# A context covariance and a value projection computed inside the third attention, and root tables loaded ahead of their use

## The reference

```python
x = x + _L2_xattn_ref(_layernorm(x), ctx_768, ctx_768, ...)   # 16 heads of 8
x = x + _L2_ffn_ref(_layernorm(x), ...)                       # top 2 of 8 experts
x = x + _L3_xattn_ref(_layernorm(x), ctx_768, ...)
...
def _L3_xattn_ref(q, k, Wq, Wk, Wv, Wo):
    query = q @ Wq.T
    key_p = k @ Wk.T
    value = k @ Wv.T
    sim = jnp.einsum('bqd,bkd->bqk', query, key_p)
    mean = jnp.mean(sim, axis=(1, 2), keepdims=True)
    var = jnp.var(sim, axis=(1, 2), keepdims=True)
    sim = (sim - mean) * jax.lax.rsqrt(var + EPS)
    attn = jax.nn.softmax(sim, axis=-1)
    out = jnp.einsum('bqk,bkd->bqd', attn, value)
    return out @ Wo.T
```

## Time and profile before

| | us |
|---|---|
| median of 3 runs (lowest to highest) | 3944.25 (3941.36 to 3946.58) |
| the profiled execution | 3943.8 |
| its span | 3942.1 |
| TensorE busy | 3643.4 (92%) |
| ScalarE busy | 2589.0 (66%) |
| VectorE busy | 1717.8 (44%) |
| GpSimd busy | 465.9 (12%) |

### The profile page before, as it was taken

How to read it: one execution, slowest core, us unless ns; L and a number is a source line. 1 busy time by engine, 2 the same in 40 slices (tenths; PEclk the granted TensorE clock), 3 DMA queues, 4 the chain that set the end, 5 groups by cost and what they waited for, 6 DMA issues and landing times.

```text
span 3942.1 us, 83687 instructions
## 1 busy us (share of the span) xinstructions
PE 3643.4 (92%) x30692; PEld 1378.2 (35%) x30692; DVE 1717.8 (44%) x1661; ACT 2589.0 (66%) x2756; POOL 465.9 (12%) x1844
## 2 busy tenths in 40 slices
PE   7999999999899999999999999868888888798989
PEld 4333333345433333333333333421111111455444
DVE  4222222223377777777777777710000000543344
ACT  5999999973355655555555555479999999102321
POOL 1222222210000000000000000012222222100210
PEclk8999999999899999999999999989999999898989
DMA  5323232212111111111111100140101000100000
GB/s 179 102 78 101 80 99 82 95 72 64 51 33 38 43 37 38 37 42 39 38 37 41 40 27 1 43 121 4 38 3 38 3 3 1 47 21 1 0 12 27
DMA packets 109875, 183.11 MB, mean 46 GB/s; under 512 B 23700, under 2 KB 46896, under 8 KB 107408
## 3 DMA queue, kind: packets, MB, share of 16 engines
q1 hardware_dynamic: 109584, 178.75, 14.8%
HBM read 107.13 MB, written 71.57 MB: 45 GB/s over the span
## 4 chain that ended last, share of the span: by engine, by line
PE 71%; ACT 12%; issue 11%; DVE 4%; ACTq 1%; DMA 0%; SPq 0%; POOLq 0%; DVEq 0%; POOL 0%
PE ps L672 18%; PE ps L697 18%; ACT probs L1014 12%; PE ps L463 7%; PE ps L451 4%; PE ps L432 3%; PE ps L576 3%; PE ps L555 2%; PE ps L830 2%; PE ps L841 2%; PE ps L437 2%; PE ps L889 2%; PE ps L903 1%; PE ps L562 1%; PE ps L257 1%
## 5 line engine op out<-in xcount | busy, mean ns | idle before, releaser
L1014 ACT ACTIVATE probs<-ps 128x1024 f32<-128x1024 f32 x1632 | 1512.4, 1083 | 60.3 <-PE ps L451 60.1
L1111 ACT ACTIVATE probs<-ps 128x1024 f32<-128x1024 f32 x816 | 836.4, 1025 | 596.4 <-PE ps L672 583.5
L1743 DVE TENSOR_TENSOR vbuf<-vbuf,probs 128x1024 f32<-128x1024 f32 (+1 forms) x800 | 972.9, 1223 | 335.5 <-ACT probs L1111 335.5
L463 PE MATMUL ps<-probs,vst 128*32 128x512 f32 x6528 | 864.8, 602 | 137.5 <-ACT probs L1014 137.3
L451 PE MATMUL ps<-qz,kst 32*128 32x512 f32 x3264 | 415.3, 495 | 25.8 <-issue 19.9
L451 PEld LDWEIGHTS ps<-qz,kst 32*128 32x128 f32 x3264 | 162.6, 182 | 712.7 <-issue 689.3
L1264 POOL CAST kst<-kb 128x128 fp32r x816 | 241.9, 296 | 1289.2 <-PE ps L463 1178.2
L1570 DVE COPY qs<-ps 128x512 f32<-128x512 f32 (+1 forms) x208 | 141.6, 681 | 574.3 <-PE ps L437 285.2
L672 PE MATMUL ps<-probs,kb 64*64 64x512 f32 x2560 | 332.3, 589 | 0.0
L1609 DVE COPY work<-ps 128x512 f32 x16 | 11.1, 692 | 694.9 <-PE ps L463 694.9
L672 PE MATMUL ps<-probs,qz 64*64 64x512 f32 x2048 | 269.8, 594 | 8.2 <-issue 7.9
(11 more groups left out here) (366 smaller groups left out, 3091.9 us busy)
## 6 DMA issues: line engine op xcount, KB each, us to landing
kv_scratch<-qs SPq DMA_DIRECT2D x192, 256.0 KB, 2.0
kb<-k_scratch SPq DMA_DIRECT2D x24, 816.0 KB, 7.3
kb<-kv_scratch SPq DMA_DIRECT2D x72, 256.0 KB, 2.9
qz<-kv_scratch SPq DMA_DIRECT2D x64, 256.0 KB, 2.9
k_scratch<-klo SPq DMA_DIRECT2D x24, 512.0 KB, 3.4
vbuf<-in_L_ffn_W SPq DMA_DIRECT2D x32, 256.0 KB, 3.1
klo<-kv_scratch SPq DMA_DIRECT2D x32, 256.0 KB, 2.9
qs<-kv_scratch SPq DMA_DIRECT2D x24, 256.0 KB, 3.0
```

The source lines that it names most:

```text
L463: mm = pe.matmul(ps[32 * j:32 * j + 32, 6 + half, :], vst[:, r, 32 * j:32 * j + 32], probs[:, r, j * HT:(j + 1) * HT], start=start, stop=stop)
L1014: act.activation(probs[:, r, b * T:(b + 1) * T].rearrange("p (h n) -> p h n", h=2), ps[:, 2 * buf:2 * buf + 2, :], ACT.Exp, scale=HD8 ** - ...
L1111: act.activation(pr1[:, (u + 2 * odd) % 4], ps[:, 2 * b:2 * b + 2, :], ACT.Exp, scale=HD64 ** -0.5)\
L1743: dve.tensor_tensor(sum1[0:k, odd, h], sum1[0:k, odd, h], e, ALU.add).then_inc(s["added"], 1)
```

## The change

Three things are done.

1. The mean of the context is spread in step 3 of half 6 of the third attention (the first half of the last group of heads). VectorE copies and subtracts it there, in three pieces of 17, 17 and 16 tiles and one of 4 rows, and GpSimd does so no longer. TensorE computes the covariance in steps 16 to 48 of the same half, one or two tiles in a step, each as three matmuls with 32 columns of weights, in bank 7. The load of the context is issued by SyncE after the queries of half 7, and `cn2` lies in the buffer of keys that the last group doesn't use.
2. The value projection is computed in half 7, in 26 parts of up to 256 context rows, each tile as four matmuls with 32 columns of weights, in bank 6; VectorE copies the 13 chunks out, where ScalarE did so.
3. `load_table(5, ACT.Sqrt)` stands at six further places of ScalarE's program, behind the exps and activations that use other tables.

Beside this the loop over the groups of the third attention is unrolled in TensorE's and VectorE's programs.

```diff
+COV_FROM = 16
+COV_AT = [COV_FROM + k * (ST - 2 - COV_FROM) // ST for k in range(ST)]
+V3_PARTS = 2 * NC
+V3_AT = [RING, RING] + [2 * RING + k * (ST - 2 * RING) // (V3_PARTS - 2) for k in range(V3_PARTS - 2)]
...
+CENTRED = 2 * NG - 2
...
-        cmean = flat[:, 5 * T:5 * T + C]
+        cmean = klo[:, 0, 0:C]
...
-        cn2 = vbuf[:, 2 * T:2 * T + ST * C].rearrange("p (t c) -> p t c", t=ST)
+        cn2 = kbf[:, 0:ST * C].rearrange("p (t c) -> p t c", t=ST)
...
-        vp = vbuf[:, 0:ST * P]
+        vp = kbf[:, 0:ST * P]
...
+                def context_mean(gh):
+
+                    pe.wait_ge(s["den_copied"], gh + DENS[layer])
+                    pe.wait_ge(s["x_ready"], 4)
+                    pe.matmul(ps[:, 7, 0:P], stat[:, 0:1].to_broadcast([P, P]), ident[:, :], start=True, stop=True)\
+                        .then_inc(s["cmean_ready"], 1)
+
+                def covariance(t):
+
+                    pe.wait_ge(s["ccent_ready"], min(3, t // PIECE + 1) if t < SF else 4)
+                    k = P if t < SF else TAIL
+                    for j in range(C // 32):
+                        cut = slice(32 * j, 32 * j + 32)
+                        mm = pe.matmul(ps[cut, 7, 0:C], cn2[0:k, t, cut], cn2[0:k, t, :], start=(t == 0), stop=(t == ST - 1))
+                    if t == ST - 1:
+                        mm.then_inc(s["cov_ready"], 1)
+
+                def values3(gh, c, p0, p1):
...
+                    if c == 0 and p0 == 0:
+                        pe.wait_ge(s["den_copied"], gh + DENS[layer])
+                    if c and p0 == 0:
+                        pe.wait_ge(s["v3_copied"], c)
+                    for u in range(p0, p1, P):
+                        for j in range(G):
+                            cut = slice(32 * j, 32 * j + 32)
+                            mm = pe.matmul(ps[cut, 6, u:u + P], ctxT[0:C, c0 + u + 32 * j:c0 + u + 32 * j + 32], wT[0:C, 3, :],
+                                           start=True, stop=True)
...
+                        elif g * 2 + half == CENTRED + 1:
+                            pe.wait_ge(s["cov_copied"], 1)
...
+                            elif gh == CENTRED:
+                                if t == RING:
+                                    context_mean(gh)
+                                for k in range(ST):
+                                    if COV_AT[k] == t:
+                                        covariance(k)
+                            elif gh == CENTRED + 1:
+                                for k in range(V3_PARTS):
+                                    if V3_AT[k] == t:
+                                        values3(gh, k // 2, k % 2 * (HT // 2), (k % 2 + 1) * (HT // 2))
...
-            pe.matmul(ps[:, 5, 0:P], stat[:, 0:1].to_broadcast([P, P]), ident[:, :], start=True, stop=True)\
-                .then_inc(s["cmean_ready"], 1)
...
             exps8(0)
+            load_table(5, ACT.Sqrt)
             layernorm(1)
...
             exps8(2)
+            load_table(5, ACT.Sqrt)
             layernorm(5)
...
+            load_table(5, ACT.Sqrt)
             experts8(1)
...
             exps1(3, mode3, 0, stat[:, 12:13])
+            load_table(5, ACT.Sqrt)
             layernorm(8)
...
-            pool.wait_ge(s["in_ctx2"], 32)
-            pool.wait_ge(s["cmean_copied"], 1)
-            pool.tensor_tensor(cn2[:, 0:SF, :], cn2[:, 0:SF, :], cmean.unsqueeze(1).to_broadcast([P, SF, C]), ALU.subtract)\
-                .then_inc(s["ccent_ready"], 1)
-            pool.tensor_tensor(cn2[0:TAIL, SF, :], cn2[0:TAIL, SF, :], cmean[0:TAIL], ALU.subtract).then_inc(s["ccent_ready"], 1)
...
+                def centred_context():
+
+                    dve.wait_ge(s["cmean_ready"], 1)
+                    dve.tensor_copy(cmean, ps[:, 7, 0:C]).then_inc(s["cmean_copied"], 1)
+                    dve.wait_ge(s["in_ctx2"], 32)
+                    dve.wait_ge(s["cmean_copied"], 1)
+                    for t0 in range(0, SF, PIECE):
+                        t1_ = min(SF, t0 + PIECE)
+                        dve.tensor_tensor(cn2[:, t0:t1_, :], cn2[:, t0:t1_, :],
+                                          cmean.unsqueeze(1).to_broadcast([P, t1_ - t0, C]), ALU.subtract).then_inc(s["ccent_ready"], 1)
...
+                def move3(c):
+
+                    c0, wd = CHUNKS[c]
+                    dve.wait_ge(s["v_proj"], 2 * NVG + c + 1)
+                    dve.tensor_copy(vp[:, c0:c0 + wd], ps[:, 6, 0:wd]).then_inc(s["v3_copied"], 1)
...
+                sp.dma_start(cn2[:, 0:SF, :], whole).then_inc(s["in_ctx2"], 16)
+                sp.dma_start(cn2[0:TAIL, SF, :], rows[SF * P:S, :]).then_inc(s["in_ctx2"], 16)
```

More of the change, by code:

```diff
@@ L530, in attention8 @@
                     else:
[L531 to L533 removed]
+                        for g in range(NG):
+                            group(g, 0)
                 with pe.Else():
@@ L789, in _ @@
             mm.then_inc(s["sum_ready"], 1)
-            pe.wait_ge(s["ccent_ready"], 2)
-            for t in range(ST):
-                k = P if t < SF else TAIL
-                mm = pe.matmul(ps[0:C, 2, 0:C], cn2[0:k, t, :], cn2[0:k, t, :], start=(t == 0), stop=(t == ST - 1))
-            mm.then_inc(s["cov_ready"], 1)
             layernorm(7)
@@ L1610, in attention8 @@
                             .then_inc(s["acc_copied"], 1)
+                if n == 0:
+                    with dve.Fori(0, NG // 2) as gi:
+                        halves8(gi)
+                else:
+                    for gi in range(NG // 2):
+                        halves8(gi)
                 normalise8(2 * NG - 1, 1)
```

58 lines of the change are left out of this document (29 added, 29 removed).

## The result

| | before | changed |
|---|---|---|
| median of the runs | 3944.57 us (3941.36 to 3946.58, 4 runs) | 3909.72 us (3909.62 to 3913.53, 3 runs) |
| the profiled execution | 3943.8 | 3909.72 |
| its span | 3942.1 | 3908.0 |

The ratio is 0.9916, with a 95% interval of 0.9896 to 0.9935: faster, by some 33 us or 0.8%. One further execution of the changed kernel (5321.4 us), in which TensorE's granted clock had a mean of 0.65, is left out of the table. The forecast was 3922.8, with a range of 3918 to 3930. The direction was right, and the gain was about 1.6 times the forecast one.

What follows compares the result with a forecast made beforehand. Three streaming attentions, with short serial parts between them, were taken to bound the kernel. Gains of 25.35 us less 3.9 of cost left 21.45, so 3943.8 became 3922.35, or 3922.8 as the runs' median; range 3918 to 3930.

Steps and rivals of the forecast that it cites:

- (1): Layernorm after the third attention: the context mean's matmul no longer stands ahead of it on TensorE, 0.3 us gained.
- (2): Same layernorm: without GpSimd's subtraction VectorE's add no longer waits its turn, 10.0 us gained, bounds 9.0 and 10.1.
- (3): Layernorm behind the experts: with the covariance gone it starts 4.9 us earlier; 2.55 us gained, bounds 2.5 and 4.9.
- charge of 2.35 us: Layernorm behind the experts: TensorE's clock falls in the 3.9 us pause, costing 2.35 us up to the next projection.
- (4): Before the last attention: the ones matmul no longer waits behind the value projection, 12.1 us gained, bounds 11.5 and 12.7.
- (5): Layernorm roots: earlier table loads gain about 0.1 us at each of four places, 0.4 us, bounds 0 and 0.6.
- (6): Third attention's last two halves: moved work costs 3.9 us (covariance 0.5, context mean 0.3, staging 2.2, double value part 0.9).
- my rivals: Nothing meets or cools 3918.3 (0.18); thin cover 3932.0 (0.16); whole loads 3918.1 (0.03); no change 3944 (0.02); slower 3961 (0.01).

Runs made afterwards that it cites:

- second profile: The changed kernel run once more, unaltered: five runs with a median of 3911.26 us, ratio 0.9923, span 3909.5 us.

## Why the prediction was wrong, point by point

- **What bounds the kernel**: right. The work in the attention cost at most 2.8 us, and work taken out of the serial parts came back in full.
- **(1), (2), mean and subtraction**: right. The add went from 11.31 to 1.22 us, and the stage lost 10.96 against 10.5 forecast. In the kernel where the work was left out it lost 12.8, with the second layernorm's means warm, so this size has some 2 us of clock in it too: the variant with small subtractions, warm there as well, lost 13.0.
- **(3), covariance**: the wait and the cold start came as described (3.87 us, 3.55 us), but the size was off: 7.01 (and 4.0 in the second profile) where I had 2.55. L247 starts 4.9 us earlier, as forecast. The charge of 2.35 us for the cold layernorm up to the next projection came out as 1.3 (in the second profile as 2.45), and the two steps from there to the matmul by the covariance, which I put at nothing, gave 3.4 (in the second profile 1.6). I compared a cold layernorm with the one of before up to the next projection and took it that everything behind stays as it was. But before was itself cold from there on, L803 at 3.75 us. With the pause in front the clock fell earlier, and it was up again before the first projection in seven of nine profiles and before the second in all. The row was in front of me; I charged the clock's fall and didn't ask when it would rise again.
- **(4), values**: right, 12.62 and -0.38 where I had 12.7 and -0.6. What no term held is the 1.4 us that the cold first scores cost behind it (6.63 us for 5.26). The idle time in front can't be the whole reason, as the run with matmuls there had 6.37.
- **(5), root tables**: the mechanism was right where loads are hidden, and one place of four had a second effect, through the clock, of 1.75 us, of which the last attention took most back (1.25). The Trainium skill (page ScalarE: Activation LUTs, section "What ACT_TABLE_LOAD costs") gives 2.66 us for a switch, half of it a drain after the load. This case doesn't show the drain: without the loads the root of the last layernorm begins at 3765.99, 0.01 us after a load of 1.28 us has ended, and six loads fewer or more made 1.1 us of span.
- **(6), costs**: 2.76 where I had 3.9. The meeting of GpSimd and VectorE happened, in turns; it was felt for 1.4 us, not 2.2, and the covariance sets cost nothing where I had 0.5.
- **The sentence that failed most**: "The unrolled loop of the third attention adds instructions in a branch that is not taken." I gave it no cost and no bounds. It was worth 5.6 us here, and could have been minus 3.5. The stalls were in the trace of before (9.23 and 3.50 us, "issue"), and I hadn't read the rows between the attention's bound and its first step, because no moved work stood there.
- **The range**: 25.35 less the cost, 21.45, is 6.0 short of what the moved work gave in its own rows (10.96 + 7.01 + 12.62 - 0.38 - 2.76 = 27.45), and 4.4 of that is term (3). With the start (5.6) and the layernorm (4.4) added to the 21.45, and 1.1 less cost, 32.5 are there; the remaining 1.6 are small differences in the other rows, of which only the last layernorm's 1.75 us was traced. Without the start's 5.6 us, which were luck, the time would have been some 3915, below the range as well. None of my rivals held a gain over 26 us, since all of them argued on the listed edits.

What stays open: what sets the granted clock in the stages between the attentions. The same program met it in different places, and a difference of 3 us between two single profiles there means nothing by itself. The kernel before ran between 3932.34 and 3950.36 in the runs beside these experiments.

## What to carry to other kernels

A change that alters the length of an engine's code can move its stalls for instructions, even if the added code never runs; look for "issue" in front of the first instruction behind a branch, compare the time over it by itself, and try the usual branch first, judging it at the stage's end: it gained at the start of all three attentions here, and only in the third did more of that remain than its end took. Where one engine's work is to lie beside another's small copies, cut it into instructions as short as those copies' slack. And in a serial stretch follow TensorE's clock to the point where it is the same in both kernels, not only to the next matmul.

## What the runs showed of the hardware

- Instructions arrive by DMA in packets of some 16 KB. Behind the jump over the branch not taken, TensorE's first matmuls in the third attention waited 8.1 to 9.9 us while other loads held over 90% of the DMA engines; 3.4 to 3.7 us of that it waits without the jump too, for GpSimd. Jumps at the ends of attentions went with waits of 1.7 to 3.3 us. A second wait of 3.5 to 8.5 us followed in four profiles: after the first two scores matmuls in one, in the third group of scores in the three others.
- VectorE's subtraction from SBUF and GpSimd's copies take turns by whole instructions: copies of 0.22 and 0.29 us became 1.83 and 1.82 beside pieces of 1.8 us, and 0.45 to 0.64 beside pieces of 0.6. The Trainium skill's page SBUF — State Buffer, section "Who interferes with whom", says that a VectorE instruction with two SBUF inputs and a GpSimd instruction that reads SBUF exclude each other; the trace agrees, and adds that the length of the single instruction sets the price.
- A pause of 3.87 us in front of the layernorm left it cold in nine of nine profiles where it wasn't filled, at 3.42 to 3.78 us for 1.98. Filled, it was warm at first (1.98), and L262 (2.79 us for 2.05) and L849 (3.75) show the clock falling, 5 to 9 us behind the add.
- Three matmul groups of 32 columns beside each other, and four, took no time that was felt: 51 sets and 26 parts in halves of 94.22 us.
